# A fused transformer decoder: TensorE's attention step with the projections first and the mixing last, and the subtraction of the maxima ahead of the second scores

## What is computed

```
n      = layernorm(x)
q,k,v  = n Wq, (n or ctx) Wk, (n or ctx) Wv
s      = q k^T * scale (+ mask rows, or + relative positions)
p      = exp(s - max(s))            # L3_xattn: no softmax
x      = x + (p v / sum(p)) Wo (+ bias)
```

## Time and profile before

| | |
|---|---|
| time, median of 3 runs | 4896.48 us (4889.78 to 4901.68) |
| the profiled execution | 4900.09 us, its span 4898.2 us |
| PE busy | 4007.7 us (82%) |
| DVE, POOL, ACT busy | 3203.4, 2994.6, 2059.5 us |
| mean granted clock of PE | 0.889 of full |

### The profile page before, as it was taken

How to read it: one execution, slowest core, us unless ns; L and a number is a source line. 1 busy time by engine, 2 the same in 40 slices (tenths; PEclk the granted TensorE clock), 3 DMA queues, 4 the chain that set the end, 5 groups by cost and what they waited for, 6 DMA issues and landing times. The chain is left out here.

```text
span 4898.2 us, 215645 instructions
## 1 busy us (share of the span) xinstructions
PE 4007.7 (82%) x85067; PEld 2918.6 (60%) x85076; DVE 3203.4 (65%) x10848; ACT 2059.5 (42%) x5737; POOL 2994.6 (61%) x4949
## 2 busy tenths in 40 slices
PE   8999977254899978656999997559879998889988
PEld 6777754132566666523777774335547776667766
DVE  5875668422344688787556874753337878888866
ACT  4555545011344444365555554112225543336632
POOL 6766632276455699688556762038876777777710
PEclk9999988555899998755999997879998999999999
DMA  3000012433100022200000002113431000000000
GB/s 94 5 13 19 19 28 57 78 62 54 37 0 0 18 39 39 35 1 1 2 0 15 22 18 54 42 46 75 77 62 35 0 15 16 16 9 1 0 13 24
DMA packets 380509, 139.58 MB, mean 28 GB/s; under 512 B 216487, under 2 KB 373239, under 8 KB 380055
## 3 DMA queue, kind: packets, MB, share of 16 engines
q1 hardware_dynamic: 345430, 107.60, 9.3%
q0 software_dynamic: 34816, 28.34, 4.0%
HBM read 91.46 MB, written 43.85 MB: 28 GB/s over the span
## 5 line engine op out<-in xcount | busy, mean ns | idle before, releaser
L1051 DVE TENSOR_REDUCE rowmax<-ps 128x16 f32<-128x1024 f32 x512 | 626.3, 1223 | 488.0 <-PE ps L678 487.7
L696 PE MATMUL ps<-prob,kT 32*64 32x256 f32 x9216 | 781.7, 408 | 8.7 <-issue 2.4
L721 PE MATMUL ps<-v,probT 64*64 64x64 f32 x36864 | 764.6, 227 | 5.3 <-issue 2.2
L721 PEld LDWEIGHTS ps<-v,probT 64*64 64x64 f32 x36864 | 683.8, 140 | 57.4 <-issue 16.0
L678 PE MATMUL ps<-kblock,qT 32*64 32x256 f32 x8192 | 697.0, 410 | 17.2 <-DVE rowmax L1060 14.2
L900 ACT ACTIVATE probT<-ps 128x1024 f32<-128x1024 f32 x512 | 518.0, 1012 | 353.4 <-PE ps L708 353.0
L585 POOL TENSOR_TENSOR kblock<-kT,key_scale 128x512 f32<-128x512 f32 x576 | 599.8, 1041 | 18.2 <-ACT kT L878 7.6
L587 POOL TENSOR_TENSOR prob<-qT,key_scale 128x512 f32<-128x512 f32 x576 | 601.5, 1044 | 0.0
L561 POOL TENSOR_TENSOR vareps<-moments,eps 128x1 f32<-128x1 f32 x522 | 98.8, 189 | 745.7 <-DVE negmean L1025 745.6
L887 ACT ACTIVATE xn<-x_res,nmr,rstd 128x128 f32 (+1 forms) x512 | 252.7, 494 | 513.6 <-POOL nmr L567 349.5
L708 PEld LDWEIGHTS ps<-mT,pick_bf 32*64 32x64 bf16 x16384 | 311.7, 108 | 221.2 <-ACT mT L857 74.1
(11 more groups left out here) (380 smaller groups left out, 9655.7 us busy)
## 6 DMA issues: line engine op xcount, KB each, us to landing
ctxT<-in_ctxT SPq DMA_DIRECT2D x256, 64.0 KB, 1.8
held<-in_g_w SPq DMA_DIRECT2D x16, 836.0 KB
ctxT<-in_ctxT SPq DMA_DIRECT2D x256, 32.0 KB, 1.9
table<-prob SPq DMA_DIRECT2D x32, 256.0 KB, 2.4
x_dram<-x_res SPq DMA_DIRECT2D x32, 256.0 KB, 2.4
x_res<-x_dram SPq DMA_DIRECT2D x16, 512.0 KB, 6.9
x_res<-in_x SPq DMA_DIRECT2D x8, 512.0 KB, 7.5
x_res<-in_e_w SPq DMA_DIRECT2D x64, 64.0 KB
```

The costliest lines, as they stand in the source:

```text
L696: mm = nc.tensor.matmul(out.rearrange("p (h s) -> p h s", h=GH), k.kT[rows, buf, S * b:S * b + S], k.qblock[rows, buf, :, S * b:S * b + S] ...
L721: mm = nc.tensor.matmul(k.ps_o[S * b:S * b + S, u, S * hh:S * hh + S], k.probT[rows, buf, at:at + S], k.v9[rows, buf, (HD + 1) * h:(HD + 1 ...
L1051: nc.vector.tensor_reduce(spread, heads, AX.X, ALU.max).then_inc(soft.did["max_raw"], 1)
```

## The change

TensorE's step becomes B, A, D, C. The four waits before D, the wait for `exp_done` of the mixing, and A's own waits now all stand between B and A. The mixing's wait for `v_done` stands at the head of the step; `on_done` is waited for before the transpose in A. Inside D, `less_max` comes before `key_scores` in both halves: in a stage without added rows the first four `less_max` matmuls open the accumulation. ACT copies `ps_oT` and `ps_v` after `ps_mT`, `ps_xT`, `ps_q` and `ps_k` instead of before them. DVE normalises the mixed rows at the end of its step, after the maxima. The number of instructions that compute is the same.

```diff
-    def key_scores(part, buf, groups, first):
+    def key_scores(part, buf, groups):
...
-                    start=not part.softmax or first, stop=not part.softmax, tile_position=place)
+                    start=not part.softmax, stop=not part.softmax or groups == low, tile_position=place)
...
     def less_max(part, buf, h, groups):
...
-                    start=False, stop=groups == low and h == GH - 1, tile_position=place)
+                    start=groups == high and h == 0 and not part.added, stop=False, tile_position=place)
...
         mm = None
+        if mixes is not None:
+            after(pe, c, "v_done", it, mb)
+        after(pe, c, "kT_done", it, 3)
+        if c.steady is None:
+            after(pe, c, "xT_done", it, 2)
+            after(pe, c, "mT_done", it, 6)
+        if project is not None:
...
+        if norm is not None:
+            after(pe, c, "xn_done", it, 1)
+            mm = nc.tensor.transpose(k.ps_xT, k.xn[:, b1, :], k.ident)
+        if less is not None:
+            after(pe, c, "max_done", it, 5)
+            mm = nc.tensor.matmul(k.ps_mT, top_halves(k.rowmax[:, b5, :]), k.ident_bf[:, :], start=True, stop=True)
+        if mm is not None:
+            mm.then_inc(c.front_psum, 1)
+
+        mm = None
+        if score1 is not None:
+            after(pe, c, "max_done", it, 4)
+            after(pe, c, "kblock_done", it, 3)
+        if score2 is not None:
+            after(pe, c, scores_read(c, it, 6), it, 6)
+            after(pe, c, "qblock_done", it, 5)
+        if mixes is not None:
+            after(pe, c, "exp_done", it, mb)
         if value is not None or turn is not None or out is not None:
             after(pe, c, values_read(c, it, 4), it, 4)
             after(pe, c, "y_read", it, 9)
             after(pe, c, "oT_done", it, 8)
         if out is not None:
             mm = nc.tensor.matmul(k.ps_y, k.oT[:, b8, :], weights(out, 3), start=True, stop=True)
+        if mixes is not None and turn is None:
+            after(pe, c, "on_done", it, mb + 1)
...
         if score2 is not None:
-            mm = key_scores(score2, b5, high, first=not score2.added)
             if less is not None:
                 after(pe, c, "mT_done", it, 5)
                 for h in range(GH):
-                    mm = less_max(less, b5, h, high)
+                    less_max(less, b5, h, high)
+            mm = key_scores(score2, b5, high)
             mm.then_inc(score2.did["first_rows"], 1)
...
             after(pe, c, "first_rows", it, 5)
-            mm = key_scores(score2, b5, low, first=False)
             if less is not None:
                 for h in range(GH):
-                    mm = less_max(less, b5, h, low)
+                    less_max(less, b5, h, low)
+            mm = key_scores(score2, b5, low)
             mm.then_inc(score2.did["s2_psum"], 1)
+
+        if mixes is not None:
+            for hh in range(HEADS // 2):
+                mm = mix(mixes, (par - mb) % NB, hh)
+            mm.then_inc(mixes.did["o_psum"], 1)
```

More of the change, by code:

```diff
@@ L725, in mix @@
         return mm
[L727 to L739, removed]
     def step(it, par):
@@ L769, in step @@
             mm.then_inc(c.yv_psum, 1)
[L771 to L781, removed]
-        early = less is None or any(part is not None and part.added for part in (score1, score2))
-        if less is None:
-            values_mixable(mixes, it, mb)
-            scores_writable(score1, score2, it)
-        if norm is not None:
-            after(pe, c, "xn_done", it, 1)
-            mm = nc.tensor.transpose(k.ps_xT, k.xn[:, b1, :], k.ident)
-        if less is not None:
-            values_mixable(mixes, it, mb)
-            if early:
-                scores_writable(score1, score2, it)
-            after(pe, c, "max_done", it, 5)
-            mm = nc.tensor.matmul(k.ps_mT, top_halves(k.rowmax[:, b5, :]), k.ident_bf[:, :], start=True, stop=True)
-        if mm is not None:
-            mm.then_inc(c.front_psum, 1)
-        if mixes is not None:
-            for hh in range(HEADS // 2):
-                mm = mix(mixes, (par - mb) % NB, hh)
-            mm.then_inc(mixes.did["o_psum"], 1)
-        if not early:
-            scores_writable(score1, score2, it)
         for bk in range(2):
@@ L878, in step @@
                 nc.scalar.activation(k.kT[:, b2, :], k.ps_k, ACT.Copy).then_inc(project.did["kT_done"], 1)
+        if turn is not None:
+            act.wait_ge(c.yv_psum, it - 2)
+            after(act, c, "y_read", it, 8)
+            if c.name(it, 3) in VALUE_BIAS:
+                after(act, c, values_read(c, it, 3), it, 3)
+            nc.scalar.activation(k.oT[:, b7, :], k.ps_oT, ACT.Copy).then_inc(turn.did["oT_done"], 1)
+        if value is not None and value.name not in VALUE_BIAS:
+            act.wait_ge(c.yv_psum, it - 2)
+            after(act, c, "y_read", it, 8)
+            after(act, c, "o_psum", it, 3 + NB)
+            nc.scalar.activation(values(k, b3), heads_of(k.ps_v), ACT.Copy).then_inc(value.did["v_done"], 1)
         if plain is not None:
@@ L1071, in step @@
                                     ALU.add).then_inc(plain.did["exp_done"], 1)
+        mixes, mb = c.mixing(it)
+        if mixes is not None and mixes.softmax:
+            inv = k.rowinv[:, :].rearrange("p (u h e) -> p u h e", u=2, e=1)
+            sums = mixed(k)[:, :, :, HD:HD + 1]
+            after(dve, c, "o_psum", it, mb)
+            if mixes.name == "L1_xattn":
+                nc.vector.tensor_scalar(inv, sums, 1e-30, None, ALU.max).then_inc(mixes.did["sum_done"], 1)
+                after(dve, c, "sum_done", it, mb)
+                nc.vector.reciprocal(k.rowinv[:, :], k.rowinv[:, :]).then_inc(mixes.did["inv_done"], 1)
+                after(dve, c, "z_stored", it, mb + NB, each=32)
+            else:
+                nc.vector.reciprocal(inv, sums).then_inc(mixes.did["inv_done"], 1)
+            after(dve, c, "inv_done", it, mb)
+            nc.vector.tensor_tensor(k.o[:, (par - mb) % NB, :].rearrange("p (u h d) -> p u h d", u=2, d=HD),
+                                    mixed(k)[:, :, :, 0:HD], inv.broadcast_to([P, 2, HEADS // 2, HD]),
+                                    ALU.mult).then_inc(mixes.did["on_done"], 1)
     c.run(dve, step)
```

32 lines of the change are left out of this document (5 added, 27 removed).

## The result

The changed kernel takes 5145.9 us (median of 4 runs, 5141.9 to 5157.9) against 4897.55 us of the kernel before (4 runs, 4889.8 to 4901.7): a ratio of 1.0513 with a 95% interval of 1.0490 to 1.0536. That is 248 us slower; 208 were forecast (5105 us, range 4955 to 5205). TensorE's granted clock was 0.889 of full in the profiled execution before and 0.885 in this one, far too little a difference for 5%.

The account below looks back on a forecast made before the run. PE was taken to bound the L0_attn step, with other engines close behind. Step differences of the attentions times 64 tiles summed to 208 us, added to the 4896.5 us median: about 5105 us, range 4955 to 5205.

Parts of the forecast that it names:

- The likeliest case: The forecast itself: the kernel gets slower by 208 us, to about 5105 us; chance 0.55.
- Loop 2: From block A through D's reduction and both maxima splits, held by POOL's products, back to A: 5.21 us in L0_attn.
- loop-boundary stretch: Longer steps, about every fourth in L0_attn, making the mean 4.55 us against 4.43; taken as hidden after the change.
- Loop 1: From block A through DVE, POOL and ACT to the exponential's end and back to A: 4.70 us, 5.29 in L3_ffn.
- rival (d): Slower still, 5203 us: L3_ffn at 5.78, L1_xattn at 0.76, and 0.1 a step in six attentions; chance 0.10.
- upper bound of 5.78: L3_ffn's step in us if POOL's two products catch both maxima splits; 5.29 was taken instead.
- L2_attn, +0.05 forecast: L2_attn's step, with the same locks as L0_xattn but no values' bias: 0.05 us longer, 3 us in all.
- Loop 3: DVE's normalisation of the mixed rows, behind the maxima, to block A's transpose: costed at nothing, with a bound of 0.1.
- L1_attn, +0.07 forecast: L1_attn's step: no loop closes, one more switch of the array's form costs 0.07 us, 5 us in all.
- L1_xattn +0.3: L1_xattn's step, set by DVE and POOL: 0.3 us longer between bounds of 0 and 0.76, 20 us in all.
- Rival (a): Only the exponential's loop closes, as at most one maxima split is caught by POOL: 67 us slower, 4963 us; chance 0.20.
- Rival (b): Faster: the wait before L794 goes and nothing replaces it, 93 us less, 4803 us at the most; chance 0.10.

Follow-up runs that it names:

- the version at 4860 us: The changed kernel with the waits moved to where first needed and DVE's normalisation between the two splits of the maxima: 4860.1 us, 0.9927 of the kernel before.

## Why the prediction held, and where it did not

The likeliest case came: slower, inside the range, by the mechanism named. That the total is only 40 us off is in part luck. By the steps times 64 the forecast is 75 us short (283 for 208), 54 of them in L3_ffn and L2_attn; but the product itself is 25 us larger than what was measured in the trace, and the changed kernel's trace is some 10 us above its median. Step by step:

- *Loop 2 sets L0_attn, L2_xattn and L3_attn*: right. With the splits out of POOL's products these three fell, with the exponential's waits late they did not. Its size was 0.1 short: 5.32 in the step shown for 5.21. Between A's last matmul (to 206.11) and x_res (206.26) lie 0.15 us where 0.06 was taken. L0_xattn has the same locks (the splits take 0.23 and 0.96 us in the mean, and end with the two products) and the same missing 0.1: +0.25 forecast and +0.35 measured.
- *The loop-boundary stretch "taken as hidden"*: wrong. In L0_attn the steps go 5.28, 5.35, 5.51, 5.34 and again, 5.37 in the mean. The one of 5.51 is the turn of the kernel's loop (those that end in A's loads near 135, 157 and 178 us): there A's load comes 0.22 behind the second split and not 0.05.
- *Loop 1 at 4.70*: the term of the sum that was most mis-sized. Its handover is not 0.06 but 0.44, the passing of seven other waits, and with 1.15 for 1.06 the loop is 5.17 us. The 0.06 was read in a place where the exponential's wait is the last: in that step of the kernel before, the trace has it on L794's load itself. The prediction had 0.1 for handing over the waits, and only in rival (d). In the three attentions above this was covered by loop 2. In L3_ffn it was not: A to the sum 1.16, then 4.18 to the exponential's end, 0.47 to A, in all 5.81 where 5.29 was forecast. So it is in 31 of 43 steps (5.78 in the mean). In the other 12 both splits are caught by both products, as the upper bound of 5.78 had it, and the step is 5.91. One of the 31 steps of L3_ffn in the changed kernel's timeline (answers to the earlier trace rows):

```profile
4757.20 0.29 DVE L982 TENSOR_TENSOR held<-held,ps 128x128 f32 x1 [1.08 <-PE ps L785]
...
4759.71 0.17 DVE L1031 TENSOR_TENSOR rowmax<-rowmax 128x16 f32<-128x16 f32 x1
4759.81 1.04 POOL L585 TENSOR_TENSOR kblock<-kT,key_scale 128x512 f32<-128x512 f32 x1
4759.92 0.96 DVE L1034 TENSOR_TENSOR rowmax<-rowmax 128x16 f32<-128x16 f32 x1
4760.38 1.00 ACT L890 ACTIVATE probT<-ps 128x1024 f32<-128x1024 f32 x1
...
4761.85 0.30 PEld L773 LDWEIGHTS ps<-attn_w,oT 128*128 128x128 f32 x2 [1.17 <-DVE rowmax L1034]
```

  L1031 passes just ahead of `kblock` and L1034 is held by `kblock` alone, exactly as forecast, and is done at 4760.88. The product isn't delayed by the split that runs ahead of it: it starts 2.61 us after the sum (2.59 before) and takes its 1.04. The profile still names L1034 as the releaser, which ended 0.97 before A; the exponential ends at 4761.38.
- *L2_attn, +0.05 forecast and +0.37 measured*: the locks were there, but not side by side with both products. The added rows delay the reduction, so the first split starts in `qblock` and lasts to its end, and the second follows behind: from x_res 4.05 to `qblock`'s end, 0.24 for the second split, 0.05 to A, 1.16 to the next x_res, together 5.50. Rows of that step in L2_attn, whose loads of A lie 5.51 apart:

```profile
2565.64 0.30 PEld L773 LDWEIGHTS ps<-attn_w,oT 128*128 128x128 f32 x2 [0.64 <-DVE rowmax L1034]
...
2566.80 0.29 DVE L982 TENSOR_TENSOR x_res<-x_res,ps 128x128 f32 x1 [0.71 <-PE ps L785]
...
2569.81 1.04 POOL L587 TENSOR_TENSOR prob<-qT,key_scale 128x512 f32<-128x512 f32 x1
...
2569.87 1.02 DVE L1031 TENSOR_TENSOR rowmax<-rowmax 128x16 f32<-128x16 f32 x1
...
2570.92 0.18 DVE L1034 TENSOR_TENSOR rowmax<-rowmax 128x16 f32<-128x16 f32 x1
...
2571.15 0.30 PEld L773 LDWEIGHTS ps<-attn_w,oT 128*128 128x128 f32 x2 [0.60 <-DVE rowmax L1034]
```

- *Loop 3 at nothing*: right for the changed kernel, where loop 2 covers it (the normalisation ends at 205.55 and the transpose loads at 205.72), and nothing was lost by it in the sum. But it was not as short as that sounds: about 5.15, level with loop 1's 5.17 behind loop 2. It took the gain of the late waits.
- *L1_attn, +0.07 forecast and -0.17 measured*: the sign was wrong, and so was "L1_attn keeps its step" among the signs to look for. In the kernel before, L794 stood 30.0 us idle in 88 pieces in a window of 44 steps, half of the pieces the weight load's and half the matmul's, all put down to "issue":

```profile
L794 PE MATMUL ps<-ident_bf,rowmax x44: 216/216/217, 1360.1 to 1639.4; 128*128 128x128 bf16 x44
...
  issue: 30.0, 88
```

  That is the passing of waits in the middle of TensorE's queue; of the 30.0 us the matmuls' 44 pieces are 10.4, 0.24 us of idle PE a step. In three steps of four the last signal, that of the maxima, comes 0.27 us before L794's load, and two more wait instructions lie between; in the fourth all waits were satisfied, and four such instructions are passed all the same. In the changed kernel the same operation has no such idle time, and the wait instructions stand beside the loads of q and k (1502.41 to 1502.79 in one step), while matmuls are in hand. This was read off, not tested. PE's idle time fell from 0.24 to 0.03 us a step and the step by 0.17, which leaves some 0.04 of longer work where the forecast had 0.07 for one more change of the array's form.
- *D unchanged, L1_xattn +0.3, L3_xattn 0, no cost of the order itself*: D's order as expected in the new place (1.69 us, reduction 1.48 after its start), L1_xattn +0.28, L3_xattn +0.01; and the version at 4860 us has the new block order. In L1_xattn the 0.3 was an estimate between bounds of 0 and 0.76. That the place of the normalisation has a part in it shows in the 6.15 and 6.18 us with the normalisation between the splits; how the 0.28 come about was not looked into.
- *Rival (a)*, that only loop 1 closes, is nearly what the splits ahead of the reduction produced: 5071 us and not 4963, a good part of the difference being the passing of waits (93 us came back with their order). Rival (b)'s gain does exist, 38 us of its 93, once the waits stand late and the normalisation is moved too.

## What to carry to other kernels

A wait should stand at the first instruction that needs it. Gathered ahead of the first block of a step, waits turn loops that had one step and a half into loops of one step, and the longest of these becomes the period. When several loops lie within a few tenths, opening one shows only the next: draw up all of them with their lengths first, and look at what stands in the queue behind an operation that is held.

Of several waits at one place, the signal that comes last should be the last one waited for. The order in the kernel's text need not be that of the queue: here the wait written first ended up last, on the load, in three steps of four. And a releaser that the profile names should be checked against its end, and against what the instruction really waits for.

## What the hardware showed that was not expected

- Waits cost time after the last signal has come: TensorE's satisfied wait instructions take 0.051 us and stand 0.11 apart, with one or two semaphores each, and with the late signal first of eight waits A's load came 0.42 to 0.44 us after it, with the late signal last 0.05. Ordering them, and leaving out one that stood twice, was worth 93 us of 5071.
- A 128x16 `tensor_scalar` of DVE from SBUF to SBUF is held by a running POOL product as long as a `tensor_tensor` (633 and 632 ns in the mean); the same subtraction takes 0.17 us when POOL is not in its products.
- The reciprocal and the normalisation, which read PSUM, ran beside POOL's product unheld: 0.24 us for the reciprocal and 0.29 for the normalisation with L587 in progress.
